# Attention values as the weights: 32 columns of values loaded, the transposed probabilities streamed, in a two-layer gated cross-attention network

## The reference

```python
x = x + tanh(g_xattn[0]) * attention(layernorm(x), ctx)        # no mask
x = x + tanh(g_ffn[0])   * experts(layernorm(x))               # 4 experts of 256, 1 to 4 of them per token
x = x + tanh(g_xattn[1]) * attention(layernorm(x), ctx, mask)  # one 64x64 mask
x = x + tanh(g_ffn[1])   * conv_ffn(layernorm(x))              # ternary weights, 3-tap convolution, silu
```

```python
p   = softmax(q @ k.T / sqrt(8))     # 64 x 64
out = p @ v                          # 64 x 8
```

## Time and profile before

| | us |
|---|---|
| median of 3 runs | 943.17 (941.88 to 944.72) |
| profiled execution, its own time | 943.28 |
| span of the profiled execution | 941.5 |
| TensorE passes in flight (PE) | 913.9, 97% of the span, 11654 passes |
| TensorE weight loads (PEld) | 737.7, 78% |
| VectorE (DVE) | 810.5, 86%, 2348 instructions |
| ScalarE (ACT) | 763.4, 81%, 1675 |
| GpSimd (POOL) | 664.4, 71%, 1254 |
| DMA, mean rate over the span | 33 GB/s |

### The profile page before, as it was taken

One profiled execution on the slowest core, in us unless ns is written; L12 is line 12 of the kernel. 1 busy time (PEld: TensorE's weight loads), 2 busy tenths in 40 slices (PEclk: granted clock), 3 DMA queues, 4 the chain that ended last, 5 costly groups with the idle time before them and its releaser, 6 DMA issues. The chain is left out here.

```text
span 941.5 us, 32708 instructions
## 1 busy us (share of the span) xinstructions
PE 913.9 (97%) x11654; PEld 737.7 (78%) x11654; DVE 810.5 (86%) x2348; ACT 763.4 (81%) x1675; POOL 664.4 (71%) x1254
## 2 busy tenths in 40 slices
PE   6999999999999999999899999999999999999996
PEld 3888888878889999998786777777777777777774
DVE  6888888899979989889788888888887869999996
ACT  5888888888887777777567787878878889999995
POOL 5787777776536556556989777676765558889883
PEclk9999999999999999999999999999999999999998
DMA  3501011100000000000000000000000003333343
GB/s 116 187 25 47 25 47 37 36 25 14 14 2 1 2 1 1 1 2 1 1 14 13 26 13 14 25 14 26 14 26 2 4 18 76 72 76 77 74 72 82
DMA packets 54272, 31.17 MB, mean 33 GB/s; under 512 B 38368, under 2 KB 46816, under 8 KB 54112
## 3 DMA queue, kind: packets, MB, share of 16 engines
q1 hardware_dynamic: 54112, 29.08, 11.9%
HBM read 16.48 MB, written 4.19 MB: 22 GB/s over the span
## 5 line engine op out<-in xcount | busy, mean ns | idle before, releaser
L997 DVE TENSOR_REDUCE smax<-score 128x16 f32<-128x1024 f32 x128 | 156.7, 1224 | 63.4 <-DVE a_st L992 38.9
L1365 PEld LDWEIGHTS bank<-vb,prob_t 128*64 128x64 f32 x4096 | 130.3, 138 | 49.8 <-issue 41.7
L1006 DVE TENSOR_TENSOR prob<-score,smax 128x512 f32<-128x512 f32 x256 | 164.9, 686 | 0.8
L642 ACT ACTIVATE prob_t<-bank 128x512 f32<-128x512 f32 x256 | 139.1, 596 | 19.8 <-PE bank L1340 5.9
L637 ACT ACTIVATE prob<-prob 128x512 f32<-128x512 f32 x256 | 147.5, 631 | 5.7 <-DVE prob L1006 5.7
L1365 PE MATMUL bank<-vb,prob_t 128*64 128x18 f32 x4096 | 142.6, 212 | 0.1
L1340 PE MATMUL bank<-const,prob 128*128 128x128 f32 x1024 | 133.1, 273 | 0.7 <-DVE x_all L1107 0.7
L1340 PEld LDWEIGHTS bank<-const,prob 128*128 128x128 f32 x1024 | 115.7, 141 | 1.6 <-DVE x_all L1107 1.1
L721 ACT ACTIVATE eb_t<-eb,gwt 128x128 f32<-128x128 f32 x256 | 81.4, 390 | 39.6 <-POOL eb_acc L494 26.0
L648 ACT ACTIVATE o_t<-bank,b_col 128x128 f32<-128x128 f32 x128 | 48.7, 380 | 66.2 <-PE bank L1340 65.9
L428 POOL TENSOR_SCALAR kj<-k_sb,const 128x512 f32<-128x512 f32 x124 | 85.2, 694 | 21.8 <-issue 21.8
(11 more groups left out here) (169 smaller groups left out, 2363.4 us busy)
## 6 DMA issues: line engine op xcount, KB each, us to landing
ctx_t<-in_ctx SPq DMA_DIRECT2D x32, 256.0 KB, 2.7
x_all<-in_x SPq DMA_DIRECT2D x16, 256.0 KB, 3.7
out_x<-x_all SPq DMA_DIRECT2D x64, 64.0 KB, 1.8
ew<-in_ew SPq DMA_DIRECT2D x2, 512.0 KB, 6.1
q2t<-q2b SPq DMA_TRANSPOSE x64, 2.5
f_cw<-in_f_cw SPq DMA_DIRECT2D x1, 768.0 KB, 7.5
w_t<-in_w_attn SPq DMA_DIRECT2D x2, 256.0 KB, 4.1
f_w<-in_f_w SPq DMA_DIRECT2D x2, 256.0 KB, 6.8
```

The source lines that it names most:

```text
L642: act.activation(prob_t[:, 4 * half:4 * half + 4, :].rearrange("p i q -> p (i q)"), bank[(PT, PT2)[half]], ACT.Copy).then_inc(s["p_copied" ...
L997: dve.tensor_reduce(smax[:].rearrange("p (r h) -> p r h", r=RH), sc, AX.X, ALU.max).then_inc(s["smax_done"], 1)
L1006: dve.tensor_tensor(prob[:, par, half * 512:(half + 1) * 512].rearrange("p (r h k) -> p r h k", r=2, k=S), sc[:, g], m.unsqueeze(3).to_bro ...
L1365: last = pe.matmul(bank[OV][q, i * 2 * VW:(i + 1) * 2 * VW], prob_t[:, i, q], vb[:, k // G, v0 + b * NPAIR + i, :, :].rearrange("p h v -> ...
```

## The change

`values` exchanges the two sides. `vb` now holds, per sequence and per four heads, blocks of 32 columns, of which 16 are the values of two heads and 16 are zero. A matmul loads 32 columns of `vb` as weights and streams 64 columns of `prob_t`; two of them accumulate (`q` = 0, 1) into 32 partitions of the result, so that the four `r` fill 128 partitions: the result stands with the head and value on the partitions and the queries as columns, which is what the output projection needs as weights. The ones are gone from `vb`; eight more matmuls, with 32 columns of a new constant block (`C_DEN`) as weights and 128 columns of `prob_t` streamed, add up the probabilities and put each sum on the 8 partitions of its head. `divide` takes 128 reciprocals per partition instead of 16 and writes `o_t` directly. `transpose_o`, `copy_o`, `o_n` and its semaphores go; `project_o` and `residual` move one step earlier (n-3). `values(n)` now waits for `residual(n-2)` and, ahead of its first matmul, for both halves of `prob_t`. The bias of the values, so far added by `copy_o`, goes through the output projection once per layer (`project_bv`) and is folded into `bo_row` by `scale_bo`, which now waits for it; that of layer 1 moves into the experts. `vb` is cleared by POOL, as its second instruction, and has 4096 columns instead of 2304. The three tails lose the same steps.

```diff
-        o_tr_ps, wo_ps = bank[OV][:, 2 * P:3 * P], bank[OV][:, 3 * P:4 * P]
+        ov_ps, den_ps, wo_ps = bank[OV][:, 0:P], bank[OV][:, P:2 * P], bank[OV][:, 3 * P:4 * P]
...
-        vb = sb("vb", [P, 2, G * BT * NPAIR, 2, VW])
+        vb = sb("vb", [P, 2, G * BT * RH, 4, 2 * HD])
...
             pool.memset(zeros[:], 0.0).then_inc(s["zero_set"], 1)
+            pool.memset(vb[:].rearrange("p a g q v -> p (a g q v)"), 0.0).then_inc(s["vb_set"], 1)
...
-                    if has(-3):
-                        copy_o(L, n - 3)
                     if has(-1):
                         copy_p(n - 1, 0)
                         copy_p(n - 1, 1)
...
             def scale_bo(L):
-                dve.tensor_scalar(bo_row[:, L, :], bo_row[:, L, :], tg[:, L:L + 1], None, ALU.mult)\
+                dve.wait_ge(s["bv_mm"], L + 1)
+                dve.scalar_tensor_tensor(out=bo_row[:, L, :], in0=bo_row[:, L, :], scalar=tg[:, L:L + 1],
+                                         in1=bank[(PT2, PT)[L]][:, 0:P], op0=ALU.mult, op1=ALU.add)\
                     .then_inc(s["setup_v"], 1)
...
-            def divide(n, k):
-                ov = bank[OV][:, 0:H * VW].rearrange("p (h v) -> p h v", h=H)
+            def divide(n):
+
                 wait(dve, "pv_mm", n + 1)
-                wait(dve, "o_copied", n)
+                wait(dve, "wo_mm", n)
                 wait(dve, "o_norm", n)
-                dve.reciprocal(rden[:], ov[:, :, HD]).then_inc(s["rden_done"], 1)
-                wait(dve, "rden_done", n + 1)
-                dve.tensor_tensor(o_n[:, k % 2, :].rearrange("p (h v) -> p h v", h=H), ov[:, :, 0:HD],
-                                  rden[:].unsqueeze(2).to_broadcast([P, H, HD]), ALU.mult)\
-                    .then_inc(s["o_norm"], 1)
+                dve.reciprocal(rden[:], den_ps).then_inc(s["rden_done"], 1)
+                dve.wait_ge(s["rden_done"], n + 1)
+                dve.tensor_tensor(o_t[:].rearrange("p (s b) -> p b s", b=BT), ov_ps.rearrange("p (b s) -> p b s", b=BT),
+                                  rden[:].rearrange("p (b s) -> p b s", b=BT), ALU.mult).then_inc(s["o_norm"], 1)
...
                     if has(-2):
-                        divide(n - 2, k)
-                    if has(-4):
-                        residual(n - 4, t - 4)
+                        divide(n - 2)
+                    if has(-3):
+                        residual(n - 3, t - 3)
...
+            def project_bv(L):
+
+                pe.wait_ge(s["wo_scaled"], L + 1)
+                pe.matmul(bank[(PT2, PT)[L]][:, 0:P], b_col[:, L, 2:3].to_broadcast([P, P]), w_t[:, L, 3, :],
+                          start=True, stop=True).then_inc(s["bv_mm"], 1)
...
                 wait(pe, "o_norm", n)
-                wait(pe, "x_attn", n - 2)
-                wait(pe, "o_copied", n - 1)
-                for i in range(NPAIR):
-                    if i % 4 == 0:
-                        wait(pe, "p_copied", 2 * n + i // 4 + 1)
-                    for b in range(BT):
-                        q = slice(b * S, (b + 1) * S)
-                        last = pe.matmul(bank[OV][q, i * 2 * VW:(i + 1) * 2 * VW], prob_t[:, i, q],
-                                         vb[:, k // G, v0 + b * NPAIR + i, :, :].rearrange("p h v -> p (h v)"),
-                                         start=True, stop=True, skip_group_check=True)
+                wait(pe, "x_attn", n - 1)
+                wait(pe, "p_copied", 2 * n + 2)
+                for b in range(BT):
+                    t = slice(b * S, (b + 1) * S)
+                    for q in range(2):
+                        for r in range(RH):
+                            pe.matmul(ov_ps[32 * r:32 * r + 32, t],
+                                      vb[:, k // G, v0 + b * RH + r, 2 * q:2 * q + 2, :].rearrange("p q v -> p (q v)"),
+                                      prob_t[:, 2 * r + q, t], start=(q == 0), stop=(q == 1), skip_group_check=True)
+                for q in range(2):
+                    for r in range(RH):
+                        last = pe.matmul(den_ps[32 * r:32 * r + 32, :], const[:, C_DEN + 32 * q:C_DEN + 32 * q + 32],
+                                         prob_t[:, 2 * r + q, :], start=(q == 0), stop=(q == 1), skip_group_check=True)
                 last.then_inc(s["pv_mm"], 1)
 
-            def transpose_o(n, k):
-                wait(pe, "o_norm", n + 1)
-                tr(o_tr_ps, o_n[:, k % 2, :]).then_inc(s["o_tr"], 1)
...
-                    if has(-4):
-                        project_o(L, n - 4)
                     if has(-3):
-                        transpose_o(n - 3, (k - 3) % 8)
+                        project_o(L, n - 3)
```

More of the change, by code:

```diff
@@ L38 @@
 ROUND = 1.5 * 2.0 ** 23
-C_ID, C_ONE, C_J, C_H, C_TIE, C_THR, C_POW, C_RND, C_EPS, C_NEG, C_ID2, C_NRND = \
-    0, 128, 256, 264, 266, 282, 285, 286, 287, 288, 289, 417
-C_ALL = 418
+C_ID, C_ONE, C_J, C_H, C_TIE, C_THR, C_POW, C_RND, C_EPS, C_NEG, C_ID2, C_NRND, C_DEN = \
+    0, 128, 256, 264, 266, 282, 285, 286, 287, 288, 289, 417, 418
+C_ALL = 482
 def build(nc, a, out):
@@ L643, in copy_p @@
                                bank[(PT, PT2)[half]], ACT.Copy).then_inc(s["p_copied"], 1)
[L645 to L651, removed]
             def split_qk_weights(L):
@@ L961, in masks, with residual @@
                 dve.tensor_scalar(neg_mask[:], m_keep[:], 1.0, NEG, ALU.subtract, ALU.mult).then_inc(s["mask_v"], 1)
-            def residual(n, t, read=None):
+            def residual(n, t):
                 wait(dve, "wo_mm", n + 1)
-                wait(dve, "o_copied", n + 2 if read is None else read)
                 wait(dve, "bo_added", n + 1)
                 dve.tensor_tensor(x_tile(t), wo_ps, x_tile(t), ALU.add).then_inc(s["x_attn"], 1)
-            def divide(n, k):
-                ov = bank[OV][:, 0:H * VW].rearrange("p (h v) -> p h v", h=H)
+            def divide(n):
                 wait(dve, "pv_mm", n + 1)
-                wait(dve, "o_copied", n)
+                wait(dve, "wo_mm", n)
                 wait(dve, "o_norm", n)
-                dve.reciprocal(rden[:], ov[:, :, HD]).then_inc(s["rden_done"], 1)
-                wait(dve, "rden_done", n + 1)
-                dve.tensor_tensor(o_n[:, k % 2, :].rearrange("p (h v) -> p h v", h=H), ov[:, :, 0:HD],
-                                  rden[:].unsqueeze(2).to_broadcast([P, H, HD]), ALU.mult)\
-                    .then_inc(s["o_norm"], 1)
+                dve.reciprocal(rden[:], den_ps).then_inc(s["rden_done"], 1)
+                dve.wait_ge(s["rden_done"], n + 1)
+                dve.tensor_tensor(o_t[:].rearrange("p (s b) -> p b s", b=BT), ov_ps.rearrange("p (b s) -> p b s", b=BT),
+                                  rden[:].rearrange("p (b s) -> p b s", b=BT), ALU.mult).then_inc(s["o_norm"], 1)
             def attention(L):
@@ L1206, in attention0_tail @@
                 relu(0, 0, 1)
-                divide(n - 1, n - 1)
-                residual(n - 3, n - 3)
+                divide(n - 1)
+                residual(n - 2, n - 2)
                 dve.wait_ge(s["thr_done"], 1)
@@ L1212, in attention0_tail @@
                 relu(0, 0, 3)
-                divide(n, n)
-                residual(n - 2, n - 2)
+                divide(n)
+                residual(n - 1, n - 1)
                 gate_counts(0)
                 gate_select(0)
-                residual(n - 1, n - 1)
                 gate_weigh(0)
@@ L1222, in attention0_tail @@
                 group_stats(3, 1)
-                residual(n, n, n + 1)
+                residual(n, n)
                 relu(0, 0, 7)
@@ L1318, in attention1_tail @@
                 n, t = 2 * T - 1, T - 1
-                divide(n - 1, n - 1)
-                residual(n - 3, t - 3)
+                divide(n - 1)
+                residual(n - 2, t - 2)
                 lead_in(ffn, 0, 0)
-                divide(n, n)
-                residual(n - 2, t - 2)
+                divide(n)
                 residual(n - 1, t - 1)
+                residual(n, t)
                 lead_in(ffn, 1, 1)
-                residual(n, t, n + 1)
             dve.wait_ge(s["sc_set"], 2)
@@ L1347, in transpose_p @@
                 wait(pe, "p_copied", 2 * n + half - 1)
+                if half and n == 0:
+                    pe.wait_ge(s["setup_v"], 1)
                 for i in range(4):
@@ L1488, in beside_first_scores @@
             def beside_first_scores():
+                pe.wait_ge(s["q_ready"], G)
+                project_bv(0)
                 pe.wait_ge(s["a_xn_ready"], 2 * G)
@@ L1630, in _ @@
             attention0_tail()
+            pe.wait_ge(s["p_copied"], 2 * T)
+            project_bv(1)
             run_tiles(pe, experts, 1, 0, T=NG, first=1)
-            pe.wait_ge(s["wo_scaled"], 2)
+            pe.wait_ge(s["setup_v"], 2)
             pe.wait_ge(s["w1_in"], 16)
@@ L1705, in attention1_tail @@
                 conv_tap(1, 0)
-                wait(pe, "o_norm", n + 1)
-                project_o(1, n - 1)
```

(6 more changed lines are left out.)

48 lines of the change are left out of this document (14 added, 34 removed).

## The result

The changed kernel takes **979.88 us** (median of 4 runs, 978.53 to 980.57) beside 942.54 for the kernel before (also of 4): ratio 1.0389, 95% interval 1.0375 to 1.0403. The forecast was 932.7 us with a range of 925 to 970. The span grows from 941.5 to 978.0 us.

A forecast was written before the change was run, and what follows sets the result against it. TensorE was taken to bound three tiles of four, a score-bank loop the short one. Layer 0 -6.2 and +1.9, layer 1 -6.2, together -10.5 us, gave 932.7 us against the median, range 925 to 970.

The forecast's parts named there:

- the price of the reciprocal: VectorE's reciprocal, 16 to 128 columns: +0.12 us, paid in one tile of four of layer 0, +1.9 us in all.
- the slow reciprocal: Rival, 5%: reciprocal +0.74 us, VectorE at 4.17 us per tile bounds layer 0, +23, a little more in layer 1: 968 us.
- The mask: Layer 1: mask matmuls ahead of the scores, 0.33 us from their load to the scores' load, cover the longer reciprocal.
- The bound: TensorE bounds three tiles of four; the short tile's score-bank loop, 3.52 us in layer 0, stays whatever TensorE saves.
- TensorE's terms: Values and denominators, four passes at a time, 0.91 us instead of 0.93; transpose gone, 0.11: saving 0.13 us per tile.
- the sum: Layer 0: -6.2 for 48 tiles, +1.9 for the reciprocal in 16; layer 1: -6.2; together -10.5 us.
- The tile for which I saw no slack: Layer 0, the tile after the short one: values wait for product and residual, so the reciprocal gives back 0.12 us.
- The rival that column groups do not overlap: 18%: 32-column shapes also run two passes at a time on TensorE, +97 us, 1040 us.
- the rival on the weight loads: 8%: TensorE's weight loads do not run beside the stream at 32 columns, +24 us, 967 us.
- a forecast of 0 between -1.2 and +1.5: Start of the kernel: POOL's clearing of the values and VectorE's relief there change the time by 0 us.
- the first of the two prices: POOL clearing 4096 columns at VectorE's price, 1.98 us for 2304, ends near 4.3 us, before POOL's first work at 4.95.
- ScalarE's lost copies: 128 copies of the transposed output, 0.38 us each, go from ScalarE; nothing gained by itself, since it waited for TensorE.

The follow-up runs named there:

- the run with 64 columns: The changed kernel with the reciprocal on 64 of the 128 columns: 946.62 us, ratio 1.0039.
- the exchanged transposes: The changed kernel with the transposes of the probabilities ahead of the values in TensorE's step: 972.40 us, ratio 1.0313.
- With 16 columns: The changed kernel with the reciprocal on 16 of the 128 columns: 933.63 us, ratio 0.9902.
- the run that puts all passes into one group: The changed kernel with 16 reciprocal columns, all 24 matmuls of a tile writing the first 32 partitions of their result: 1255.12 us, ratio 1.3323.
- the run with exp(-ln): The changed kernel with ScalarE making the reciprocal as exp(-ln(sum)), projection behind the transposes, activation tables loaded: 930.45 us; without hand-loaded tables 1210.13 us.

## Why the prediction was wrong

**The step that failed** is the price of the reciprocal: "I take VectorE's usual rate, 1.23 us for 1024, 112 more columns, +0.13, rounded down for its fixed part to +0.12". It measured +0.70, 112 columns of 6.25 ns. The upper bound of that step, 0.74, was within 6%, and its row was in hand: 4 columns in 168 ns and 16 in 247 are 6.6 ns per column of this very operation. I gave the row of another operation more weight than two rows of the right one, because one of the two reads PSUM. The Trainium skill would have spoken for the dear end: "VectorE: DVE Perf Modes", section "First, the fixed hardware budget", calls the reciprocal an iterative divide with a repeat count of 8. It gives no time; the runs agree in kind, with 6.25 ns per column where the row maximum pays 1.2.

**The rival that came true** is the slow reciprocal, at a chance of 5%, which was too little for an end of the range with the only rows of the same operation behind it. Its mechanism held: VectorE's 4.17 us per tile bound layer 0, +23 by the working, +24.3 measured. That the 4.17 came out to the digit is luck: the working has 3.43 and 0.74, the traces 3.47 and 0.70. Its price of 968 us was 12 short, mostly in layer 1: "a little more" was 10.5 us. That VectorE must be full on the mean of the tiles for the reciprocal to cost was the error: the run with 64 columns shows the chain through the residual costing first, and the exchanged transposes show 5.7 of the 10.5 us as TensorE standing at the values with other work behind them. The mask, which was to cover the reciprocal in layer 1, covers 0.30 us in two tiles of four (3.95 with 16 and with 64 columns), but not 0.70.

**The bound.** Right: the short tile of each group stays at 3.52 and 3.87 us in every kernel of the table with the old order, whatever TensorE saves.

**TensorE's terms.** Right in mechanism and size. Four passes side by side were taken from the share of columns, and the values and denominators cost what was forecast. With the reciprocal at its old price the three tiles that TensorE bounds save 0.12, 0.13 and 0.03 us in layer 0 and 0.13, 0.15 and 0.13 in layer 1, for 0.13 each in the sum; 943.1 to 933.6 is -9.5 us where the sum without its reciprocal term has -12.4. The tile for which I saw no slack, the one behind the short one, has none: with 64 columns the whole 0.30 us stand in it. The one that gained 0.03 is the tile of 4.14, for which the sum has the full saving. With 16 columns its values start 0.71 us behind its scores (126.48 to 127.19), just after a residual (126.66 to 126.94), where 0.62 stood before (113.02 to 113.64). That it is the residual which holds them is a reading; the 0.20 us that 64 columns add there speak for it. The rival that column groups do not overlap fell twice: by the trace, and by the run that puts all passes into one group. So did the rival on the weight loads: in the changed kernel 32 loads with the same rows run in 0.52 us beside their passes (load row at 114.43), and in the run with one group passes follow 0.057 us apart although each has a load of 110 ns of its own. The rule of the Trainium skill, "TensorE: Matmul & The Clock Gate", Part 3, that a load overlaps only where the row groups differ, is not borne out by these (the same Part also lets a load go ahead into a background weight buffer).

**The rest.** The first scores start at 12.72 us instead of 12.36, +0.36 for a forecast of 0 between -1.2 and +1.5; the runs with the same start have 12.07 to 12.71, so no cause is read from it. POOL's clearing took 3.51 us and ended at 4.26, ahead of its first work at 4.94, as the first of the two prices had it (4.3). ScalarE's lost copies show no gain of their own, as forecast: ScalarE now stands idle 167 us behind TensorE's transposes. They did free the time in which the run with exp(-ln) hides the reciprocal.

## What to carry to other kernels

When a change widens an operation, take its price per column from two rows of the same operation, and only then from its neighbours: a reciprocal is not a copy. When a transposed layout saves one engine a tenth of a microsecond, look at what the other engine must now do per column, and at who has idle time for it. And between two pieces of work on one engine, the one that waits for nothing goes first, provided that nothing queued on a third engine waits for the other.

## Not expected of the hardware

The reciprocal from PSUM is linear from 16 to 144 columns: 148 ns and 6.25 ns per column, in four kernels. Four groups of 32 columns run side by side even when neighbours in the program go to the same group: 1.08 us instead of 1.03 for values and denominators, with a pass of the next line started before the last of the old one; in one group each pass of the values takes 0.057 us alone. Ln and exp in one tile cost two table loads of 1.28 us where the placement is left to itself, and none where a table with both is loaded once; the Trainium skill, "ScalarE: Activation LUTs", section "Table sets: the hidden batching unit", counts one load for such a pair, which only the run with tables by hand bears out.
